# The fourth batch's side scan begun in the experts' stage, with three chunk places of layer 1's prologue left empty

## The chip, the cores and the metric

The kernel runs on one core of a Trainium2 chip (NeuronCore: TensorE or PE for matmuls, VectorE or DVE, ScalarE or ACT, GpSimd or POOL, and SyncE or SP, which here only issues DMAs). The metric is the time of one execution on the device in microseconds; less is better. Times given are medians of several executions.

## The reference

Two layers over x of shape 8 x 512 x 128 (batches, positions, features). Each layer adds to x the product of one path s and a gate g, both computed from the layer-normed x:

```
xn = layernorm(x)
s  = ssm(xn)                       # layer 0: the scan
g  = silu(experts(xn))             # layer 0: top 2 of 8 experts, gelu
x  = x + s * g
xn = layernorm(x)
s  = attention(xn)                 # layer 1: one causal head
g  = silu(mla_and_experts(xn))     # layer 1: 16 heads, then 8 small experts
x  = x + s * g
```

The scan of layer 0 is what the change moves. For each batch, with z = sigmoid(xn Wz + bz), x_ssm = xn Wx + bx, B = xn WB + bB, C = xn WC + bC, dt = softplus(xn Wdt + bdt), and A = -exp(A_log), it runs over the 512 positions with a state of 128 x 16:

```
h   = exp(dt * A) * h + x_ssm * (dt * B)
y_t = sum over the 16 states of h * C_t
out = (y * z) Wout + bout
```

## The kernel before

The program has three stages with a barrier behind each: `route` (normalization, routing, lists of tokens), `experts0` (layer 0's experts) and `layer1`. Layer 0's scan has no stage of its own: it runs beside the others, written into their loops.

**The side scan.** One batch's scan is cut into 8 chunks of two states each (`NC = 8`, `PER = 2`), and one chunk is a row of 1024 elements per partition. Class `Scan` holds the pieces. A chunk (b, k) takes, in this order: `load_rows` twice on GpSimd's DMA queue (line 212, the rows of B and of C spread over all partitions, 512 KB each), `decay` on ScalarE (line 250, two exponentials), and on VectorE `enter` (line 291, u times B), `step` (line 298, the scan instruction), `weigh` (line 308, state times C) and, from the second chunk on, `add` (line 315, into y). Ahead of a batch's first chunk stand four projections on TensorE (`project`, line 191: dt, bc, x, z), `take_dt`, `logarithm`, `take_bc` and a store of B and C to HBM (`store_bc`); behind its last chunk `gate` (lines 320 and 323), `project_out` (line 196) and `finish` (line 327), which writes the batch's finished rows.

**In the experts' stage** the work is 78 tiles m (`NT`), two for each of 39 pieces of 256 sorted rows. Tile m is `up(m)` on TensorE (line 779), `gelu(m)` on ScalarE (line 854), the product hid on VectorE (line 925, two instructions) and, two tiles later, `down` on TensorE (line 795). `turn_rows` (line 766) transposes the rows that GpSimd gathered (line 900), eight tiles ahead. Each engine has its own loop over m, and `chunk_due` and `scan_due` say which piece of the scan goes beside which tile: chunk n starts at tile 3n - 1 (`SCAN_TILE`, `TILES_A_CHUNK`), its step one tile later, its weigh two, its add three. The decays of two chunks are done together, one tile ahead of the even one. dt of batch b is projected 12 tiles before its first chunk, bc 10, x 4; the batch before it is projected out 4 tiles behind, and z 6 tiles behind. Three batches (`SCANNED = 3`) run here; the last add of batch 2 is at tile 71.

**In layer 1** the loops run over slots, 24 to a batch, from -30 (`SLOT0`) to 217. Slots below 0 are the prologue: the expert rows of batch 0 are gathered (`gather`, line 1677), combined (lines 1703 to 1713), normed, turned and projected (lines 1301, 1413, 1309, 1314), the queries get their rope (lines 1738 to 1744) and go by DMA into `q_all` (line 1091); from slot -8 on the maxima of the scores are made (line 1286 on TensorE, line 1723 on VectorE), turned (line 1297) and sent as a row (line 1133), and with slot 0 the scores begin (line 1238). The one-head attention runs beside them (`qk1` in slot -6, `scores1` in -5, `turn1` in -3, its maxima on VectorE in line 1869, its exponentials in line 1642). `keep_clock` (line 1222) issues matmuls whose result nobody reads. The scan's chunks have one place every four slots from slot -14 on (`SCAN_START`, `SCAN_STRIDE`): chunk (3, 0) at -14, (3, 1) at -10, and so on; the projections of a batch have slots of their own in `SCAN_PIECES`. Batch 3 fetches its turned rows from HBM in slot -30, projects bc in slot -28, dt in -22, x in -17 and z in -4. Batch 2's `project_out` and `finish` stand ahead of slot -30.

Of the kernel before, what the change touches and what calls it, by code (L numbers as in the profile page):

```python
# [21 lines left out]
B, L = 8, 512  # L22
# [309 lines left out]
def route(nc, sems_of_stage, bk, c, x, xs, t):  # L332
# [6 lines left out]
    with ExitStack() as own:  # L339
# [40 lines left out]
        with nc.Block() as block:  # L380
            @block.sync
            def _(sp):
# [32 lines left out]
                for b in range(SCANNED, B):  # L415
                    sp.wait_ge(s["xnt_ready"], b + 1)
                    sp.dma_start(t["xnt_d"][b], xn_t_all[:, b * L:(b + 1) * L]).then_inc(t["late_in"], 16)
                    late += 1
# [267 lines left out]
SCAN_TILE, TILES_A_CHUNK = -1, 3  # L686


def experts0(nc, sems_of_stage, bk, c, xs, ys, t):
# [4 lines left out]
    with ExitStack() as own:  # L694
# [20 lines left out]
        def chunk_due(m):  # L715

            n, rest = divmod(m - SCAN_TILE, TILES_A_CHUNK)
            return (n // NC, n % NC) if rest == 0 and 0 <= n < SCANNED * NC else None
# [10 lines left out]
        with nc.Block() as block:  # L729
# [27 lines left out]
            def _(pe):  # L757
# [42 lines left out]
                for m in range(NT + 2):  # L800
# [14 lines left out]
                    if (b := scan_due(m - 6)) is not None and b >= 1:  # L815
                        pe.wait_ge(s["xcol_ready"], turned(m))
                        scan.project("z", beside, xn_t_all[:, b * L:(b + 1) * L])
# [96 lines left out]
            def _(dve):  # L914
                v = nc.vector
                for m in range(SCAN_TILE, NT + 2):
# [89 lines left out]
def layer1(nc, sems_of_stage, bk, bank, c, x, ys, out, t):  # L1006
# [5 lines left out]
    with ExitStack() as own:  # L1012
# [84 lines left out]
        def scan_due(slot, what):  # L1097

            for b in range(SCANNED, B):
                after, bank_of = SCAN_PIECES[scan_start(b) % SLOTS][what]  # L1100
                if slot == scan_start(b) + after:
                    return b, bank_of

        def chunk_due(slot, after):

            n, rest = divmod(slot - after - SCAN_START, SCAN_STRIDE)
            return (SCANNED + n // NC, n % NC) if rest == 0 and 0 <= n < (B - SCANNED) * NC else None
# [7 lines left out]
        with nc.Block() as block:  # L1115
            @block.sync
            def _(sp):
# [5 lines left out]
                def fetch_turned(b):  # L1123
                    if b > SCANNED:
                        sp.wait_ge(scan.s["sc_zp"], b)
                    sp.dma_start(xn_ts[:, :], xnt_d[b]).then_inc(s["xts_in"], 16)
# [79 lines left out]
            def _(pe):  # L1206
# [146 lines left out]
                scan.project_out(pe, SCANNED - 1, bk(2))  # L1353
                for slot in range(SLOT0, SLOT1):
# [21 lines left out]
                    if (at := scan_due(slot, "bc")) is not None:  # L1376
                        pe.wait_ge(s["xts_in"], 16 * (at[0] - SCANNED + 1))
                        scan.project("bc", claim(at[1], scan.s["sc_bc"], at[0] + 1), xn_ts[:])
# [144 lines left out]
            def _(act):  # L1523
# [39 lines left out]
                for slot in range(SLOT0, SLOT1):  # L1563
# [14 lines left out]
                    if (at := chunk_due(slot, -1)) is not None:  # L1578
                        scan.decay(act, *at)
# [77 lines left out]
            def _(pool):  # L1657
                link = chain_of(pool, s["pool_chain"])
                g_ = nc.gpsimd
                for slot in range(SLOT0, SLOT1):  # L1660
                    if slot == SCAN_START - 7:
                        for k in range(2):
                            for what in range(2):
                                scan.load_rows(pool, SCANNED, k, what)
                    for what, ahead in ((0, 7), (1, 5)):
                        if (at := chunk_due(slot, -ahead)) is not None and at > (SCANNED, 1):
                            if at == (SCANNED, 2) and what == 0:
                                pool.wait_ge(q_in[0], 96)
                            scan.load_rows(pool, *at, what)
# [26 lines left out]
            def _(dve):  # L1696
# [54 lines left out]
                scan.finish(dve, SCANNED - 1, bk(2))  # L1751
                for slot in range(SLOT0, SLOT1):
# [3 lines left out]
                    if (at := chunk_due(slot, 0)) is not None and at != (SCANNED, 1):  # L1756
                        scan.enter(dve, *at)
                    if (at := chunk_due(slot, 1)) is not None and at != (SCANNED, 1):
                        scan.step(dve, *at)
                    if (at := chunk_due(slot, 2)) is not None:  # L1760
                        if at == (SCANNED, 1):
                            scan.step(dve, *at)
                        scan.weigh(dve, *at)
                        if at == (SCANNED, 0):
                            scan.enter(dve, SCANNED, 1)
# [245 lines left out]
```

## Time and profile before

| | |
|---|---|
| median of 3 runs | 1284.59 us (1284.12 to 1284.82) |
| profiled execution | 1283.6 us, its span 1281.8 us |
| granted TensorE clock, mean | 0.912 of full speed |
| busy share: PE, PEld, DVE, ACT, POOL | 85%, 54%, 75%, 49%, 24% |
| routing stage | to about 66 us of the span |
| experts' stage | about 67 to 329 us |
| layer 1's prologue | 329 to 404 us |

Times in rows are microseconds from the start of the span, unless marked ns. A row of the timeline has start, duration, engine, line, operation, what is written from what, how many instructions were merged, and in brackets how long the engine had been idle before and what ended that. "issue" means that the profile shows nothing that it waited for. SPq, POOLq and ACTq are the DMA issues of these engines. The chain is the work that ended last, followed back from the end.

### The profile page before, as it was taken

How to read it: one execution, taken by the hardware profiler on the slowest of the kernel's cores; microseconds unless marked ns; L12 is line 12 of the kernel's file. 1: busy time of each engine (PE TensorE's matmuls, PEld its weight loads, DVE VectorE, ACT ScalarE, POOL GpSimd, SP SyncE). 2: the span in 40 equal slices, each digit the busy share in tenths (PEclk: the TensorE clock that was granted, in tenths of full speed). 3: DMA queues.
4: the chain of work that ended last, by engine and by line, in shares of the span. 5: the costliest groups of instructions: out<-in, count | busy, mean ns of one | idle time of the engine just before them, and what ended most of it. 6: DMA issues, size and time to landing. Idle time of an engine off the chain costs nothing.

```text
span 1281.8 us, 19217 instructions
## 1 busy us (share of the span) xinstructions
PE 1094.9 (85%) x6765; PEld 691.2 (54%) x6765; DVE 960.7 (75%) x1490; ACT 623.0 (49%) x1111; POOL 305.9 (24%) x370
## 2 busy tenths in 40 slices
PE   7669999999678877889889988989997888899976
PEld 6557787788334334544544554554464455455453
DVE  6848887897367886898797898898889877655423
ACT  2647767664223534446445554654544543353521
POOL 2075554550403201310320330041032111000000
PEclk9679999999887789899988988988898988899998
DMA  7568777674344253244324425434432520320020
GB/s 194 181 216 255 229 234 224 221 232 142 109 84 112 87 115 97 91 102 114 96 77 111 115 96 114 115 98 116 104 106 87 123 58 27 59 52 19 19 50 9
DMA packets 97069, 150.24 MB, mean 117 GB/s; under 512 B 26984, under 2 KB 55984, under 8 KB 96912
## 3 DMA queue, kind: packets, MB, share of 16 engines
q1 hardware_dynamic: 73840, 72.33, 22.5%
q0 software_dynamic: 22976, 76.43, 19.3%
q8 instruction: 56, 0.92, 0.3%
q10 hardware_dynamic: 160, 0.26, 0.1%
q14 instruction: 37, 0.30, 0.1%
HBM read 124.33 MB, written 11.54 MB: 106 GB/s over the span
## 4 chain that ended last, share of the span: by engine, by line
PE 39%; DVE 18%; issue 6%; ACT 6%; DMA 4%; POOL 1%; SPq 1%; POOLq 0%; DVEq 0%; ACTq 0%
PE bank L1238 8%; PE bank L1267 3%; DVE neg_max L1723 3%; PE bank L1318 3%; PE bank L1327 3%; PE bank L1332 3%; DMA q_all<-turned_rows 2%; PE bank L1286 2%; PE bank L1244 2%; ACT probs L1533 2%; PE bank L1322 2%; DVE sc_state L298 2%; PE bank L1246 1%; PE bank L1309 1%; DVE sc_y L315 1%
## 5 line engine op out<-in xcount | busy, mean ns | idle before, releaser
L1533 ACT ACTIVATE probs<-bank 128x1024 f32<-128x1024 f32 (+1 forms) x192 | 169.3, 882 | 286.8 <-PE bank L1244 208.3
L1723 DVE TENSOR_REDUCE neg_max<-bank 128x2 f32<-128x1024 f32 (+3 forms) x256 | 203.4, 815 | 131.3 <-PE bank L1244 88.3
L1238 PE MATMUL bank<-q_all,kk 49*128 49x512 f32 (+3 forms) x1024 | 203.8, 497 | 49.0 <-ACT probs L1533 26.7
L212 POOL DMA_DIRECT2D sc_bc_wide<-scan_bc x128 | 73.1, 572 | 445.2 <-DVE sc_ub L291 241.1
L1238 PEld LDWEIGHTS bank<-q_all,kk 49*128 49x128 f32 x1024 | 86.5, 194 | 149.9 <-ACT probs L1533 54.9
L1286 PE MATMUL bank<-kr,q_all 48*128 48x512 f32 (+3 forms) x512 | 117.3, 494 | 43.9 <-DVE neg_max L1723 43.6
L779 PE MATMUL bank<-xcol,wst 128*128 128x256 f32 x624 | 149.8, 384 | 0.6 <-ACT xcol L841 0.6
L298 DVE TENSOR_TENSOR_SCAN sc_state<-sc_a,sc_ub 128x1024 f32<-128x1024 f32 x64 | 145.9, 2280 | 0.0
L900 POOL DMA_INDIRECT xrow<-sorted_in,token_of x78 | 103.9, 1332 | 117.5 <-PE bank L766 63.3
L779 PEld LDWEIGHTS bank<-xcol,wst 128*128 128x128 f32 x624 | 114.2, 193 | 13.6 <-issue 0.9
L1267 PE MATMUL bank<-probs,vaug 128*32 128x512 f32 (+3 forms) x1024 | 97.3, 477 | 0.0
L925 DVE SCALAR_TENSOR_TENSOR hid<-bank,wst,gel 128x256 f32<-128x256 f32 x156 | 67.3, 473 | 37.3 <-issue 24.0
L1286 PEld LDWEIGHTS bank<-kr,q_all 48*128 48x128 f32 x512 | 49.1, 201 | 77.0 <-DVE neg_max L1723 61.4
L291 DVE TENSOR_TENSOR sc_ub<-sc_u,sc_bc_wide 128x1024 f32<-128x1024 f32 x64 | 77.9, 1217 | 16.5 <-DMA sc_bc_wide<-scan_bc 14.7
L1677 POOL DMA_INDIRECT expert_out<-sorted_out,slot x64 | 75.9, 1187 | 55.2 <-POOLq L138 35.2
L250 ACT ACTIVATE sc_a<-sc_dt,neg_a 128x511 f32<-128x511 f32 x128 | 84.2, 711 | 5.7 <-PEq L682 4.3
L795 PE MATMUL bank<-w,hid 128*128 x624 | 84.7, 279 | 0.5 <-DVE hid L925 0.5
L795 PEld LDWEIGHTS bank<-w,hid 128*128 128x128 f32 x624 | 77.3, 191 | 11.4 <-issue 7.1
L854 ACT ACTIVATE gel<-bank,wst 128x256 f32<-128x256 f32 x156 | 64.6, 477 | 23.1 <-PE bank L779 22.0
L308 DVE TENSOR_TENSOR sc_ub<-sc_state,sc_bc_wide 128x1024 f32<-128x1024 f32 x56 | 67.9, 1213 | 0.0
L315 DVE TENSOR_TENSOR sc_y<-sc_y,sc_ub 128x1024 f32<-128x1024 f32 x56 | 67.9, 1213 | 0.0
L1692 POOL TENSOR_SCALAR mean_sq<-ssq 128x4 f32<-128x4 f32 x8 | 6.8, 853 | 184.0 <-ACT work_b L1590 184.0
(297 smaller groups left out, 1810.7 us busy)
## 6 DMA issues: line engine op xcount, KB each, us to landing
sc_bc_wide<-scan_bc POOLq DMA_DIRECT2D x128, 512.0 KB, 4.8
wst<-in_wexp SPq DMA_DIRECT2D x39, 512.0 KB, 4.7
q_all<-q_kind SPq DMA_DIRECT2D x94, 128.0 KB, 4.3
rec_wide<-head_recips SPq DMA_DIRECT2D x31, 256.0 KB
p_t<-gates_turned SPq DMA_DIRECT2D x14, 512.0 KB, 6.5
sorted_out<-xrow SPq DMA_DIRECT2D x7, 640.0 KB, 6.5
rows_all<-in_x SPq DMA_DIRECT2D x8, 256.0 KB, 4.7
sorted_in<-rows_all SPq DMA_DIRECT2D x8, 256.0 KB, 5.5
```

What stands on the lines that cost most here:

```text
L250: last = self.nc.scalar.activation(self.v["a"][:, n % 2, j, 1:L], self.v["dt"][:, 1:L], ACT.Exp, scale=self.neg_a[:, state:state + 1])
L291: self.nc.vector.tensor_tensor(v["ub"][:], v["u"][:].unsqueeze(1).to_broadcast([P, PER, L]), v["bc_wide"][:, n % 2, 0, :, :], ALU.mult).th ...
L298: self.nc.vector.tensor_tensor_scan(merged(v["state"][:]), merged(v["a"][:, n % 2, :, :]), merged(v["ub"][:]), 0.0, ALU.mult, ALU.add).the ...
L315: self.nc.vector.tensor_tensor(v["y"][:], v["y"][:], v["ub"][:], ALU.add).then_inc(s["sc_add"], 1)
L779: last = mm(bk(inner(m)[half])[:, i * ROWS:(i + 1) * ROWS], wst[:, w % WB, half * FF + f * P:half * FF + (f + 1) * P], xcol[:, w % 3, :], ...
L795: last = mm(bk(5)[:, r * P:(r + 1) * P], hid[:, m % 4, i, r * P:(r + 1) * P], w2[:, bass.ds(e * FF + f * P, P)], start=False, stop=(f == F ...
L900: nc.gpsimd.indirect_dma_start(out=xrow[:, m, :], out_offset=None, in_=xs[0:B * L], in_offset=bass.IndirectOffsetOnAxis(ap=t["token_of"][: ...
L1238: mm(bank[1][:, par, at:at + n], kk[rows, b % 2, kt * P:(kt + 1) * P], q_all[rows, quad // 2 % 3, pair, kt * P:L].bitcast(F32), start=(at ...
L1267: last = mm(bk(4)[row:row + 32, kt * P:L], vaug[:, b % 2, kt, :], probs[:, (6 * quad + 2 * kg + pr) % RING, par, at:at + L - kt * P], star ...
L1286: mm(bank[0][:, par, at:at + n], q_all[rows, quad // 2 % 3, pair, i * P:(i + 1) * P], kr[rows, b % 2, 0:n], start=(at == 0), stop=False)
L1533: af(probs[:, slot % RING, :, 0:width], bank[1][:, :, 0:width], ACT.Exp, scale=0.125).then_inc(s["p_ready"], 1)
L1723: last = v.tensor_reduce(neg_max[:, quad % 2, pr:4:2, i], bank[0][:, :, at:at + (i + 1) * P], AX, ALU.max, negate=True)
```

## The change

- `experts0` goes on with the scan: three more chunks (`EARLY = 3`), (3, 0) to (3, 2), at tiles 71, 74 and 77, with all that batch 3 needs ahead of them, and batch 2's `project_out`, `finish` and batch 3's z at tiles 75 and 77. ScalarE's decays come in pairs, so that of (3, 3) is made there too. VectorE's loop gets one more round (to m = 80), in which the last step, weigh and add stand. TensorE waits for `sc_rows` before it projects z.
- In `layer1` batch 3's fetch, projections, store, dt, logarithm, x and z are gone; only its gate and out stay. Chunk (3, 3) takes the place of (3, 0) at slot -14; the places at -10, -6 and -2 are empty; chunk (3, 4) and all behind it are where they were. GpSimd loads two rows in slot -21 instead of four. Batch 2's `project_out` and `finish` no longer stand ahead of slot -30.
- In `route` one store of turned rows less is made (four batches instead of five).

```diff
--- before.py
+++ after.py
@@ -412,7 +412,7 @@
                 sp.wait_ge(s["biases_split"], 6)
                 for part in range(3):
                     sp.dma_start(t["bias16"][part:part + 1, :], bias_part[:, part, :]).then_inc(s["rows16_in"], 16)
-                for b in range(SCANNED, B):
+                for b in range(SCANNED + 1, B):
                     sp.wait_ge(s["xnt_ready"], b + 1)
                     sp.dma_start(t["xnt_d"][b], xn_t_all[:, b * L:(b + 1) * L]).then_inc(t["late_in"], 16)
                     late += 1
@@ -683,7 +683,7 @@
 
 
 
-SCAN_TILE, TILES_A_CHUNK = -1, 3
+SCAN_TILE, TILES_A_CHUNK, EARLY = -1, 3, 3
 
 
 def experts0(nc, sems_of_stage, bk, c, xs, ys, t):
@@ -715,7 +715,7 @@
         def chunk_due(m):
 
             n, rest = divmod(m - SCAN_TILE, TILES_A_CHUNK)
-            return (n // NC, n % NC) if rest == 0 and 0 <= n < SCANNED * NC else None
+            return (n // NC, n % NC) if rest == 0 and 0 <= n < SCANNED * NC + EARLY else None
 
         def scan_due(m):
 
@@ -814,6 +814,7 @@
                         scan.project_out(pe, b - 1, beside)
                     if (b := scan_due(m - 6)) is not None and b >= 1:
                         pe.wait_ge(s["xcol_ready"], turned(m))
+                        pe.wait_ge(scan.s["sc_rows"], b)
                         scan.project("z", beside, xn_t_all[:, b * L:(b + 1) * L])
                     if m >= 2:
                         down(m - 2)
@@ -913,7 +914,7 @@
             @block.vector
             def _(dve):
                 v = nc.vector
-                for m in range(SCAN_TILE, NT + 2):
+                for m in range(SCAN_TILE, NT + EARLY):
                     if 0 <= m < NT:
                         dve.wait_ge(s["up_psum"], m + 1)
                         dve.wait_ge(s["gel_ready"], m + 1)
@@ -1097,14 +1098,18 @@
         def scan_due(slot, what):
 
             for b in range(SCANNED, B):
+                if b == SCANNED and what not in ("gate", "out"):
+                    continue
                 after, bank_of = SCAN_PIECES[scan_start(b) % SLOTS][what]
                 if slot == scan_start(b) + after:
                     return b, bank_of
 
         def chunk_due(slot, after):
 
+            if slot - after == SCAN_START:
+                return SCANNED, EARLY
             n, rest = divmod(slot - after - SCAN_START, SCAN_STRIDE)
-            return (SCANNED + n // NC, n % NC) if rest == 0 and 0 <= n < (B - SCANNED) * NC else None
+            return (SCANNED + n // NC, n % NC) if rest == 0 and EARLY < n < (B - SCANNED) * NC else None
 
         def quad_due(slot, after):
 
@@ -1121,8 +1126,7 @@
                     sp.dma_start(xt[:, b % 3, :, :], x[b].rearrange("(j p) d -> p j d", p=P)).then_inc(s["x_in"], 16)
 
                 def fetch_turned(b):
-                    if b > SCANNED:
-                        sp.wait_ge(scan.s["sc_zp"], b)
+                    sp.wait_ge(scan.s["sc_zp"], b)
                     sp.dma_start(xn_ts[:, :], xnt_d[b]).then_inc(s["xts_in"], 16)
 
                 def maximum_rows(quad):
@@ -1350,7 +1354,6 @@
                     last.then_inc(s["rec_psum"], 1)
                     down_part(B - 2, 3, bk(5)).then_inc(s["moe_psum"], 1)
 
-                scan.project_out(pe, SCANNED - 1, bk(2))
                 for slot in range(SLOT0, SLOT1):
                     quad, j = divmod(slot + LEAD, 6)
                     if 0 <= slot < SLOTS * B:
@@ -1374,7 +1377,7 @@
                     if (at := scan_due(slot, "z")) is not None:
                         scan.project("z", claim(at[1], scan.s["sc_z"], at[0] + 1), xn_ts[:])
                     if (at := scan_due(slot, "bc")) is not None:
-                        pe.wait_ge(s["xts_in"], 16 * (at[0] - SCANNED + 1))
+                        pe.wait_ge(s["xts_in"], 16 * (at[0] - SCANNED))
                         scan.project("bc", claim(at[1], scan.s["sc_bc"], at[0] + 1), xn_ts[:])
                     if (at := scan_due(slot, "dt")) is not None:
                         scan.project("dt", claim(at[1], scan.s["sc_dtr"], at[0] + 1), xn_ts[:])
@@ -1575,7 +1578,7 @@
                         scan.take_dt(act, at[0], bk(at[1]))
                     if (at := scan_due(slot, "log")) is not None:
                         scan.logarithm(act, at[0])
-                    if (at := chunk_due(slot, -1)) is not None:
+                    if (at := chunk_due(slot, -1)) is not None and at > (SCANNED, EARLY):
                         scan.decay(act, *at)
                     if due(slot, "silu0") == 0:
                         for j in range(J):
@@ -1659,13 +1662,10 @@
                 g_ = nc.gpsimd
                 for slot in range(SLOT0, SLOT1):
                     if slot == SCAN_START - 7:
-                        for k in range(2):
-                            for what in range(2):
-                                scan.load_rows(pool, SCANNED, k, what)
+                        for what in range(2):
+                            scan.load_rows(pool, SCANNED, EARLY, what)
                     for what, ahead in ((0, 7), (1, 5)):
-                        if (at := chunk_due(slot, -ahead)) is not None and at > (SCANNED, 1):
-                            if at == (SCANNED, 2) and what == 0:
-                                pool.wait_ge(q_in[0], 96)
+                        if (at := chunk_due(slot, -ahead)) is not None and at > (SCANNED, EARLY):
                             scan.load_rows(pool, *at, what)
                     if (b := due(slot, "gather")) is not None:
                         if b == 1:
@@ -1748,21 +1748,16 @@
                     dve.wait_ge(s["silu1_ready"], (MT + 1) * b + n + 1)
                     v.tensor_tensor(hm[:, n, :], bk(at), hm[:, n, :], ALU.mult).then_inc(s["hm1_ready"], 1)
 
-                scan.finish(dve, SCANNED - 1, bk(2))
                 for slot in range(SLOT0, SLOT1):
                     quad, j = divmod(slot + LEAD, 6)
                     if 0 <= quad < QUADS:
                         reduce_maxima(quad, j)
-                    if (at := chunk_due(slot, 0)) is not None and at != (SCANNED, 1):
+                    if (at := chunk_due(slot, 0)) is not None:
                         scan.enter(dve, *at)
-                    if (at := chunk_due(slot, 1)) is not None and at != (SCANNED, 1):
+                    if (at := chunk_due(slot, 1)) is not None:
                         scan.step(dve, *at)
                     if (at := chunk_due(slot, 2)) is not None:
-                        if at == (SCANNED, 1):
-                            scan.step(dve, *at)
                         scan.weigh(dve, *at)
-                        if at == (SCANNED, 0):
-                            scan.enter(dve, SCANNED, 1)
                     if (at := chunk_due(slot, 3)) is not None and at[1] >= 1:
                         scan.add(dve, *at)
                     if (at := scan_due(slot, "gate")) is not None:
```

## Rows read from the trace of the kernel before

**Rows 1.** The page, part 1: busy time, share of the span and instructions of each engine.

```profile
PE 1094.9 (85%) x6765; PEld 691.2 (54%) x6765; DVE 960.7 (75%) x1490; ACT 623.0 (49%) x1111; POOL 305.9 (24%) x370
```

**Rows 2.** VectorE's timeline: hid of tiles 29, 35, 53, 59 and 77.

```profile
176.04 0.88 DVE L925 SCALAR_TENSOR_TENSOR hid<-bank,wst,gel 128x256 f32<-128x256 f32 x2 [3.98 <-issue]
...
196.18 0.88 DVE L925 SCALAR_TENSOR_TENSOR hid<-bank,wst,gel 128x256 f32<-128x256 f32 x2 [3.80 <-PE bank L779]
...
255.02 0.88 DVE L925 SCALAR_TENSOR_TENSOR hid<-bank,wst,gel 128x256 f32<-128x256 f32 x2 [3.98 <-issue]
...
273.34 0.88 DVE L925 SCALAR_TENSOR_TENSOR hid<-bank,wst,gel 128x256 f32<-128x256 f32 x2 [1.98 <-issue]
...
321.34 0.88 DVE L925 SCALAR_TENSOR_TENSOR hid<-bank,wst,gel 128x256 f32<-128x256 f32 x2 [1.85 <-PE bank L779]
```

**Rows 3.** ScalarE's timeline between tiles 52 and 53.

```profile
249.38 2.56 ACT L250 ACTIVATE sc_a<-sc_dt,neg_a 128x511 f32<-128x511 f32 x4
...
252.80 1.28 ACT L854 ACT_TABLE_LOAD   x1
```

**Rows 4.** The chain that ended last, 329 to 353: start, duration, what.

```profile
332.88 3.81 PE bank L191 x4
...
351.08 2.07 PE bank L191 x2
```

**Rows 5.** VectorE's timeline, 343 to 392.

```profile
343.20 0.27 DVE L1703 TENSOR_SCALAR expert_out<-expert_out,gate 128x128 f32<-128x128 f32 x1
...
346.24 0.38 DVE L1786 BATCH_NORM_AGGREGATE mv<-stats 128x2 f32<-128x6 f32 x4
...
374.84 0.69 DVE L1738 TENSOR_TENSOR q_kind<-bank,cos_q 128x512 f32<-128x512 f32 x1 [3.78 <-issue]
...
379.70 2.28 DVE L298 TENSOR_TENSOR_SCAN sc_state<-sc_a,sc_ub 128x1024 f32<-128x1024 f32 x1
...
383.15 1.28 DVE L1723 TENSOR_REDUCE neg_max<-bank 128x2 f32<-128x768 f32 x2
...
389.90 1.23 DVE L1723 TENSOR_REDUCE neg_max<-bank 128x2 f32<-128x1024 f32 x1 [2.61 <-PE bank L1244]
391.05 2.28 DVE L298 TENSOR_TENSOR_SCAN sc_state<-sc_a,sc_ub 128x1024 f32<-128x1024 f32 x1
```

**Rows 6.** The timeline of ScalarE and TensorE, 394 to 405.

```profile
394.93 0.69 ACT L1642 ACTIVATE q_kind<-bank,neg_max 128x512 f32<-128x512 f32 x1 [5.08 <-DVE neg_max L1869]
...
400.99 0.41 PE L1297 MATMUL bank<-c_ident,neg_max 128*16 128x128 f32 x1
...
404.43 1.88 PE L1238 MATMUL bank<-q_all,kk 49*128 49x512 f32 x4 [1.09 <-DMA q_all<-turned_rows]
```

**Rows 7.** The timeline of SP's queue at the ends of the first two stages.

```profile
52.78 0.59 SPq L435 DMA_DIRECT2D sin_q<-in_sin  x1
67.73 0.38 SPq L736 DMA_DIRECT2D wst<-in_wexp  x1
...
325.56 0.36 SPq L742 DMA_DIRECT2D sorted_out<-xrow  x1
329.08 0.39 SPq L1121 DMA_DIRECT2D xt<-in_x  x1
```

**Rows 8.** The page, parts 5 and 6: groups with busy, mean ns; issues with landing.

```profile
L298 DVE TENSOR_TENSOR_SCAN sc_state<-sc_a,sc_ub 128x1024 f32<-128x1024 f32 x64 | 145.9, 2280 | 0.0
L291 DVE TENSOR_TENSOR sc_ub<-sc_u,sc_bc_wide 128x1024 f32<-128x1024 f32 x64 | 77.9, 1217 | 16.5 <-DMA sc_bc_wide<-scan_bc 14.7
L308 DVE TENSOR_TENSOR sc_ub<-sc_state,sc_bc_wide 128x1024 f32<-128x1024 f32 x56 | 67.9, 1213 | 0.0
...
expert_out<-sorted_out,slot POOLq DMA_INDIRECT x64, 2.6
```

**Rows 9.** GpSimd's timeline: the last of the first eight gathers.

```profile
338.50 0.95 POOL L1677 DMA_INDIRECT expert_out<-sorted_out,slot  x1 [0.30 <-issue]
```

**Rows 10.** Stretches: length, busy of PE, PEld, DVE, ACT, POOL (instructions), clock, DMA share, GB/s.

```profile
404.00:412.00 8.00, 6.67 (x26) 3.46 (x27) 5.83 (x6) 2.20 (x3) 6.48 (x6) 0.54 0.43 133
```

## The prediction

> **What bounds the kernel now.** I read the page first for the shares: TensorE 85%, VectorE 75%, ScalarE 49% busy [rows 1]. A share says nothing of one stage, so I then read the two places that the change touches: the experts' stage (about 68 to 329 us of the span) and layer 1's prologue (329 to 404 us, up to the first scores).
>
> In the **experts' stage** I followed one instruction, the VectorE product hid of each tile (line 925, two per tile), because it is what tiles are counted by. Three starts of it that lie 24 tiles apart are tile 29 at 176.04, tile 53 at 255.02 and tile 77, the last one, at 321.34 [rows 2]. The first 24 take 78.98 us, the last 24 take 66.32 us. The first stretch holds batch 1's last six chunks, batch 2's first two, and all that prepares batch 2 (dt, bc, x, z, out). The second holds batch 2's last six chunks and then nothing of a scan. The rows inside show where it costs: before a tile whose ScalarE work has a pair of decays ahead of it VectorE sits idle, 3.98 us (tile 29), 3.80 (tile 35) and 3.98 (tile 53) where a piece of the next batch is also in the way, 1.98 us where not (tile 59) [rows 2]. The rows on ScalarE say why: around tile 53 it loads a table, runs the four decays (2.56 us), takes z, loads the gelu table back (1.28 us) and only then makes gel, after which hid can start at 255.02 [rows 3]. So this stage is set in turn by VectorE, TensorE and, at each pair of chunks, ScalarE; the scan is not free in it.
>
> In the **prologue** I read the chain that ended last. It starts with the fetch of the turned rows of batch 3, two projections (3.81 us) and ScalarE's dt, behind which the first tanh of the expert outputs stands [rows 4]. Later it runs through the projection of x (2.07 us) [rows 4], the DMA of the query rows, in which VectorE sits idle 3.78 us [rows 5], and then a to and fro between TensorE's maxima and VectorE, where the scan's instructions stand in line with the maxima [rows 5].
>
> **Experts' stage, what is added.** With batch 3 begun at tile 71, tiles 53 to 77 do what tiles 29 to 53 do today, instruction for instruction: dt at 59, bc at 61, x at 67, decays at 70, gate at 71, out at 75, decays and z at 76 and 77. So I take 78.98 for 66.32: **+12.66 us** [rows 2]. This includes the projections, ScalarE's work with its table loads (ten in the first stretch, four in the second), the store of bc on SP's queue and the row loads on GpSimd's, since today's stretch has all of them too. The new wait of z for the finished rows of batch 2 stands on TensorE at tile 77; down 75, 76 and 77 are queued behind it. The rows are finished at tile 75 on VectorE, two tiles earlier, so it costs nothing; were they late, VectorE's own queue would be, which the 12.66 counts. Two corrections. At tile 76 no rows are left to turn, so the chain to the last gel is shorter by the turning and its copy; about 0.9 us less is my estimate, from ScalarE's small gaps there. The other is the tail. Today hid 77 starts at 321.34, the last store is issued at 325.56 and layer 1 starts at 329.08 [rows 7], 7.74 us after hid. After the change VectorE still has, behind hid (0.88) [rows 2], an add, an enter, a scan step, a weigh and an add: 1.21 + 1.22 + 2.28 + 1.21 + 1.21 = 7.1 us by the means (an add is as long as a weigh) [rows 8], 8.0 us in all. Then come the barriers; I put 1.1 of the 3.5 us between the last store's issue and layer 1 down to them and the rest to the store, an estimate. That is 9.1 instead of 7.74, **+1.4**. Sum: 12.66 - 0.9 + 1.4 = **+13.2 us** until layer 1 starts. Bounds: if the two ends of the tail hide each other wholly, and tile 76 saves 1.5, 11; if nothing is saved, 14.
>
> The Trainium skill ("ScalarE: Activation LUTs", Table sets: the hidden batching unit) says to batch activations by table set, since a change of set costs a load each time. The trace agrees: 1.28 us per load [rows 3]. By that page's 1283 ns the six loads more between gelus would cost 7.7 us, if all lay on the path, and with them alone in place of the 12.66 the time would be 1285.5; the 12.66 of the rows has them in it already.
>
> **Routing stage.** One of five stores of turned rows is gone from SP's queue. SP's last issue there is at 52.78 and its first of the next stage at 67.73 [rows 7], so nothing is won: 0.
>
> **Prologue, what is removed.** (a) Fetch, bc, store, dt and logarithm are gone. The first tanh no longer waits. What is late next is the gather of expert rows: eight of them on GpSimd's queue, the last at 338.50 [rows 9], landing 2.6 us later by the median [rows 8], 341.1. From the last combine (343.20) to the aggregate (346.24) VectorE needs 3.04 us today [rows 5], so the aggregate starts at about 344.2: **-2.0**. (b) The x projection stands between the two turnings on TensorE: 2.07 us [rows 4], at 1.2 GHz. The clock came up only later, behind this work, so with less of it ahead more of the keys' product may run at the lower level; I take **-1.6**, bounds 1.0 (all of the half clock handed on) and 2.1. (c) Chunk 3's enter, step and weigh fall into VectorE's idle time before 374.84 [rows 5], at no cost; without that cover they would be 4.7 us. Its load of rows goes out right behind the gathers on GpSimd's queue and waits for nothing. But its add now stands between the second rope and the first maximum, +1.2. (d) Behind it, today's line is reduce, step, weigh, reduce: the step starts at 379.70 and the second reduce at 383.15 [rows 5]. Without them the second reduce starts when TensorE's matmuls are done, 381.8 with the 1.2 of the add in it: -1.35. The step at 391.05 [rows 5] holds back the four maxima of the other attention; ScalarE's exponentials behind them start at 394.93 [rows 6]. Without it they end with their matmuls, at about 391.5: -3.4 in all. TensorE's turning waits for those exponentials, and behind it the maxima are turned at 400.99; then DMA, and the scores at 404.43 [rows 6]. With z's projection gone too, TensorE is late next, and I get -3.7 at the turned maxima, and so at the first scores. (e) Chunk 3's place at slots -2 to 1 is empty, but TensorE and ScalarE are the chain there: nothing. The sum of (a), (b) and (d) is 2.0 + 1.6 + 3.7 = **7.3 us** won; bounds 3.5 (if (b) and half of (d) go to other waits) and 9. From slot 2 on the program is the same.
>
> **Sum.** +13.2 - 7.3 = **+5.9 us**. Against the profiled execution's own 1283.6 (span 1281.8 and 1.8 around it) this is 1289.5; the median of the runs shown is 1.0 above that execution, so 1290.5.
>
> **Rivals.**
> *VectorE is the bound of the prologue* (ends faster). Of the 17.7 us of three chunks, 5.9 each by the means, all but one enter (that one runs in idle time today) lie behind 378; less the added add that is 15.3. If each microsecond were on the path, the gain would be 2.0 + 1.6 + 15.3 = 18.9, and the time 1284.6 + 13.2 - 18.9 = 1278.9. It decides from a prologue gain above 13.2. For it: step and reduce stand back to back at 379.70 to 383.15. Against: VectorE waits for TensorE before 389.90, 2.61 us [rows 5], so part of what goes turns into such waits. Chance 0.05.
> *TensorE's clock stays up in the prologue.* At 404 to 412 it was granted 0.54 of full speed [rows 10], and the scores' first four matmuls took 1.88 us [rows 6]. If fewer waits kept it at 2.4 GHz, each such piece on the path would be shorter by 1 us; I count up to six (x's place, keys, latents, the other attention's projections, two scores), an estimate. Net 0: 1284.5. Against: the wait for the DMA before the scores stays, and so do the gaps in which the clock falls. Chance 0.10.
> *The last tiles hide the scan.* With no rows left to turn and no gather, tiles 71 to 77 might wait for nothing but VectorE; the added stage then costs 3.7 less (one stall like the 3.98 of tile 53): 1286.8. Chance 0.11.
> *The prologue gives back little.* If the query rows' DMA or TensorE at half clock takes the place of the scan, only 3.5 of 7.3 comes: 1294.3. Chance 0.14.
> *The forecast*: chance 0.60, own range 1288 to 1293.
>
> **How the numbers follow.** The likeliest is 1290.5. The range goes from 1285.5 to 1294.5: it leaves out the first rival and the second where it is whole. About 0.2% (2.6 us) is what a measurement of this kernel can tell from no change. Faster: 0.05 of the first rival and 0.02 of the second, 0.07. Within: 0.07 of the second and 0.07 of the third, 0.14. Slower: 0.79.
>
> **What would show it.** In the changed profile hid 77 should start at about 333 to 334, with stalls of 3.8 us before tile 59 and 3 to 4 before tile 77; VectorE should end the stage with sc_y, and layer 1's fetch start at 342.3. The first aggregate should lie 15.1 us behind the start of layer 1 (17.2 today), and the first scores 68 (75.35 today). I am wrong if hid 77 starts before 330, or if the first scores come more than 13 us earlier against layer 1's start than today.

## The result, and the profile after

The changed kernel takes 1296.1 us (median of 20 runs, 1282.5 to 1300.7) where the kernel before takes 1284.7 in the same series: a ratio of 1.0080, 95% interval 1.0061 to 1.0099, so about 10.3 us slower (7.8 to 12.7); the two medians lie 11.4 apart. Forecast was 5.9 slower, with a range of 1285.5 to 1294.5: the sign is right, the size forecast is a little over half of the measured one, and the time lies outside the range. All times and ratios are of fast executions; the one slow execution, of early2 below, took 1423.3 us at a granted clock of 0.72.

The page of the changed kernel, part 1, answers to [rows 1]. The instructions of TensorE and VectorE are as many as before, and all shares stay within a point:

```profile
PE 1107.1 (85%) x6765; PEld 698.9 (54%) x6765; DVE 962.5 (74%) x1490; ACT 628.0 (48%) x1116; POOL 304.4 (23%) x370
```

VectorE's timeline gives the same tiles as [rows 2]; here are tile 29, tile 53 and tile 77, and behind tile 77 the tail of the stage, which is new:

```profile
179.01 0.88 DVE L926 SCALAR_TENSOR_TENSOR hid<-bank,wst,gel 128x256 f32<-128x256 f32 x2 [3.98 <-issue]
...
257.96 0.88 DVE L926 SCALAR_TENSOR_TENSOR hid<-bank,wst,gel 128x256 f32<-128x256 f32 x2 [3.98 <-issue]
...
336.05 0.87 DVE L926 SCALAR_TENSOR_TENSOR hid<-bank,wst,gel 128x256 f32<-128x256 f32 x2 [3.10 <-issue]
336.84 1.21 DVE L315 TENSOR_TENSOR sc_y<-sc_y,sc_ub 128x1024 f32<-128x1024 f32 x1
338.15 1.22 DVE L291 TENSOR_TENSOR sc_ub<-sc_u,sc_bc_wide 128x1024 f32<-128x1024 f32 x1
339.41 2.29 DVE L298 TENSOR_TENSOR_SCAN sc_state<-sc_a,sc_ub 128x1024 f32<-128x1024 f32 x1
341.74 1.23 DVE L308 TENSOR_TENSOR sc_ub<-sc_state,sc_bc_wide 128x1024 f32<-128x1024 f32 x1
343.00 1.23 DVE L315 TENSOR_TENSOR sc_y<-sc_y,sc_ub 128x1024 f32<-128x1024 f32 x1
```

Tiles 29 to 53 take 78.95 us, for 78.98 before. Tiles 53 to 77 take 78.09 instead of 66.32. The last store and layer 1's first fetch, on SP's queue and in the whole timeline, answer to [rows 7]:

```profile
339.59 0.36 SPq L742 DMA_DIRECT2D sorted_out<-xrow  x1
...
345.68 0.39 SPq L1126 DMA_DIRECT2D xt<-in_x  x1
```

The store is issued 3.54 us behind hid 77 (4.22 before), but VectorE works until 344.23, and layer 1 starts 1.45 us behind that.

In the prologue, VectorE's timeline around the second rope answers to the fourth to sixth of [rows 5]:

```profile
389.48 0.69 DVE L1738 TENSOR_TENSOR q_kind<-bank,cos_q 128x512 f32<-128x512 f32 x1 [6.37 <-DMA q_all<-q_kind]
...
393.21 1.22 DVE L315 TENSOR_TENSOR sc_y<-sc_y,sc_ub 128x1024 f32<-128x1024 f32 x1
394.34 1.22 DVE L1723 TENSOR_REDUCE neg_max<-bank 128x2 f32<-128x1024 f32 x1
396.99 1.29 DVE L1723 TENSOR_REDUCE neg_max<-bank 128x2 f32<-128x768 f32 x2 [1.43 <-PE bank L1250]
```

The place of the scan step between two reduces is now a wait for TensorE of 1.43 us, and the add stands ahead of the first, as the prediction had it. But VectorE waits 6.37 us for the query rows.

This profiled execution took 1300.65 us, 4.5 above the median of its kernel, so its differences are not all the change's. The traces of the other runs, below, tell them apart. Here is each trace in pieces, worked out from starts in the timelines: tile 0, tiles 53 to 77, from hid 77 to the start of layer 1 (the fetch of x on SP's queue), and, counted from that start, the first aggregate (mv), the first product with cos_k (kk), the first and second rope, the first maximum, the first scores; last what remains of the span behind the first scores.

| trace | hid 0 | 53 to 77 | tail | mv | kk | rope 1 | rope 2 | maximum | scores | rest |
|---|---|---|---|---|---|---|---|---|---|---|
| before | 81.4 | 66.32 | 7.74 | 17.2 | 28.8 | 32.3 | 45.8 | 49.5 | 75.4 | 877.4 |
| again_before | 81.5 | 66.34 | 7.61 | 17.2 | 29.0 | 32.5 | 45.9 | 49.6 | 75.5 | 877.2 |
| after | 83.5 | 78.09 | 9.63 | 15.1 | 25.4 | 28.9 | 43.8 | 48.7 | 70.9 | 882.0 |
| again_after | 81.0 | 78.13 | 9.63 | 15.1 | 25.1 | 28.6 | 45.6 | 50.5 | 72.1 | 877.0 |
| guarded | 81.0 | 78.10 | 9.62 | 15.2 | 25.5 | 29.0 | 42.1 | 47.0 | 68.9 | 873.3 |
| early2 | 83.5 | 74.90 | 7.07 | 15.2 | 24.5 | 28.0 | 40.8 | 45.7 | 69.4 | 874.8 |
| early1 | 83.8 | 73.20 | 8.47 | 15.1 | 24.8 | 28.3 | 41.5 | 46.4 | 70.2 | 871.4 |
| early0 | 83.7 | 70.91 | 8.46 | 15.1 | 24.3 | 27.8 | 40.2 | 43.9 | 68.7 | 869.0 |
| short_vector | 81.4 | 77.04 | 7.43 | 15.1 | 24.7 | 28.1 | 45.0 | 49.9 | 70.4 | 874.2 |
| short_decay | 81.6 | 75.23 | 9.62 | 15.2 | 25.0 | 28.5 | 44.7 | 49.5 | 71.5 | 870.8 |
| prefetch | 84.3 | 66.32 | 7.73 | 15.0 | 25.9 | 29.4 | 42.4 | 46.1 | 73.4 | 875.6 |
| prefetch_x | 84.7 | 66.34 | 7.59 | 15.0 | 25.3 | 28.8 | 42.3 | 46.0 | 71.9 | 873.7 |

### The profile page after: what moved, and what is told of

Same layout as the page of the kernel before. It is cut to its first block, busy times and chain, and to the rows that moved or that the text cites. A ratio compares the mean times of both kernels' runs of the same rounds, so it can differ in the third digit from the quotient of the medians.

```text
span 1298.6 us, 19225 instructions
## 1 busy us (share of the span) xinstructions
PE 1107.1 (85%) x6765; PEld 698.9 (54%) x6765; DVE 962.5 (74%) x1490; ACT 628.0 (48%) x1116; POOL 304.4 (23%) x370
## 4 chain that ended last, share of the span: by engine, by line
PE 38%; DVE 19%; issue 6%; ACT 4%; DMA 4%; POOL 1%; SPq 1%; another core or an unknown queue 0%; DVEq 0%; POOLq 0%; ACTq 0%
PE bank L1242 8%; DVE neg_max L1723 4%; PE bank L1271 3%; PE bank L1322 3%; PE bank L1331 3%; PE bank L1336 2%; PE bank L1290 2%; PE bank L1326 2%; PE bank L1248 2%; DVE sc_state L298 2%; ACT probs L1536 2%; PE bank L1250 2%; DVE sc_y L315 2%; DMA q_all<-turned_rows 1%; PE bank L1313 1%
## 5 line engine op out<-in xcount | busy, mean ns | idle before, releaser
L779 PEld LDWEIGHTS bank<-xcol,wst 128*128 128x128 f32 x624 | 114.5, 194 | 13.7 <-issue 0.9
L926 DVE SCALAR_TENSOR_TENSOR hid<-bank,wst,gel 128x256 f32<-128x256 f32 x156 | 67.3, 472 | 39.5 <-issue 28.1
L795 PEld LDWEIGHTS bank<-w,hid 128*128 128x128 f32 x624 | 78.0, 193 | 15.7 <-issue 11.8
L1677 POOL DMA_INDIRECT expert_out<-sorted_out,slot x64 | 75.4, 1178 | 39.1 <-POOLq L138 20.0
```

The lines of the kernel that those rows point to most:

```text
L779: last = mm(bk(inner(m)[half])[:, i * ROWS:(i + 1) * ROWS], wst[:, w % WB, half * FF + f * P:half * FF + (f + 1) * P], xcol[:, w % 3, :], ...
L795: last = mm(bk(5)[:, r * P:(r + 1) * P], hid[:, m % 4, i, r * P:(r + 1) * P], w2[:, bass.ds(e * FF + f * P, P)], start=False, stop=(f == F ...
```

## The experiments

Each ran in five rounds beside the kernel before on the same chip; ratios are to it.

**The change and the kernel before once more** (no edit).

> The changed kernel once more, for a second trace. The account so far: tiles 53 to 77 cost 11.8 us more than before, the tail of the experts' stage 1.9, the prologue gives back 4.5, and the 3.0 us in the routing stage and the 4.7 us behind the first scores that the first trace also shows are chance (TensorE's granted clock). It expects hid 53 to hid 77 at 78.1 us, layer 1's start to the first scores at 70.9, and 877 to 880 us behind the first scores. The rival, that the change also slows the steady part of layer 1, expects 881 to 883 there again.

> The kernel before once more, for a second trace and to see what two timings of one kernel differ by. Expected: a ratio of 1.000 with an interval of some 0.003, hid 53 to hid 77 at 66.3 us, layer 1's start to the first scores at 75.4. If the part behind the first scores (877.4 us in the first trace) comes out 3 us or more otherwise here, such differences are chance; if it is 877 again, the rival of a slower steady part gains.

The change: 1.0101 (1.0052 to 1.0151). The kernel before against itself: 0.9989 (0.9953 to 1.0024), so two such series differ by 0.1% with nothing changed, and the interval is 0.35% to either side. Tiles 53 to 77, the tail and the parts up to the first rope repeat to 0.5 us. The rest behind the first scores is 877.0 in the change's second trace and 877.2 in the second of before: the 4.7 us more in the change's first trace were chance, and so were the 2.1 us by which its tile 0 started later. The rival of a slower steady part falls. The first scores were expected at 70.9 in the change's second trace and came at 72.1. Between the ropes the two traces of the change differ, 14.9 and 17.0 us, where the two of before agree on 13.45: something there is unsteady in the change.

**Both without layer 1.** Of each kernel all of layer 1 is left out, and a copy of x stands in its place. The edit, shortened:

```diff
-        layer1(nc, sems_of_stage, bk, bank, c, x, ys, out, locals())
+        sp.dma_start(out, x[0:B]).then_inc(copied, 16)      # in a block of its own
```

> The kernel before with layer 1 left out: a copy of x to the output stands in its place, so the scan's later chunks and all of layer 1 are not computed. Expected: layer 1's place starts at 329 us of the span, so some 335 us in all. It is the base of cut_after.

> The changed kernel with layer 1 left out in the same way. If the added stage time is the tiles' 11.8 and the tail's 1.9, it is 13.7 us above cut_before. My forecast had 13.2. If a part of the 16.6 us by which layer 1 starts later in the first trace were due to the routing stage's one store less, the difference would be nearer 16.6.

340.21 us (339.3 to 341.0; about 335 was expected) and 353.85 (352.8 to 356.6): **13.64 us** more. The stage's price is thus measured by itself, in time and not only in a trace, and it is the 11.8 of the tiles and the 1.9 of the tail. The routing stage has no part in it: in the traces of these two kernels tile 53 starts at 253.92 and 253.95 us, and what stands in layer 1's place 13.72 us later in the second.

**How the price is made up: fewer early chunks.** A new table gives the places; batch 3's projections and the rest are as in the change. The edit, shortened (EARLY is 0, 1 or 2; the table's row for 1 and for 2 stands behind the mark #):

```diff
-SCAN_TILE, TILES_A_CHUNK, EARLY = -1, 3, 3
+SCAN_TILE, TILES_A_CHUNK, EARLY = -1, 3, 0              # 1, 2
+PLACES = {-14: 0, -10: 1, -6: 2, -2: 3}                 # {-14: 1, -6: 2, -2: 3}, {-14: 2, -6: 3}
+                            if at == (SCANNED, max(EARLY, 1) + 1) and what == 0:
+                                pool.wait_ge(q_in[0], 96)
```

> One part of the change alone: batch 3's projections, bc store, dt, logarithm, x, u, z and batch 2's out go to the experts' stage, and all four first chunks stay in the prologue in their old places. By the rows of before (tiles 53 to 59 cost 1.8 more with dt ahead, 59 to 65 cost 0.7 more, then x, dt, gate and out some 1.5) the stage gets 3 to 5 us longer, with no tail, since hid is VectorE's last long work; the prologue gives back the 3.5 us of the tanh and of x. Expected: 0 to 1.5 us above before. If the preparation were the costly part, it would be 8 or more above.

> The change with one early chunk instead of three (the decays of two are made early): chunk 1 in the first place of the prologue, the second place empty, chunks 2 and 3 in the last two. Against early0 the stage gets one stall behind a pair of decays (2 us) and 1 to 2 us on VectorE, the prologue gives back the first scan step behind the rope, 1.4 us. Expected: 2 to 4 us above before. If each early chunk costs a third of the whole, it is about 3.8 of 11.4.

> Two early chunks, the third in the prologue's first place, the fourth in its third place. No second pair of decays is made early, so the stall of 3.1 us before tile 77 and the tail of 1.9 us aren't there. Expected: 3 to 6 us above before. The theory that the cost sits in the second pair of decays and in the tail wants a step of 5 us or more between this and the change; if cost goes evenly with chunks, it is some 7.6 above before and the step is 3.8.

Ratios 1.0019 (0.9989 to 1.0049), 1.0019 (0.9984 to 1.0053) and 1.0035 (1.0001 to 1.0069). The times alone can't tell the first two from no change. The traces can say where layer 1 starts: tiles 53 to 77 and the tail together are 74.0 us before, 79.4 with no early chunk, 81.7 with one, 82.0 with two and 87.7 with three. So the preparation costs 5.4, the first early chunk 2.3, the second 0.3 (1.7 more in the tiles, 1.4 less in the tail), and **the third 5.7** (3.2 in the tiles, 2.6 in the tail). That is the step of 5 us or more which the theory of the second pair of decays and the tail had asked for; an even price per chunk would have given 3.8. early2 was forecast at 3 to 6 above and lies at 4.5, early1 at 2 to 4 and lies at 2.4, early0 at 0 to 1.5, measured 2.4, with an interval that holds both.

Two forecasts about early0 missed. Its stage gets 5.4 us longer, not 3 to 5, of which 0.7 is in the tail, where nothing was expected. And its prologue gives back 6.7 us (75.4 to 68.7), not 3.5, although all four chunks still stand there; guarded, below, with three of them gone, gets to 68.9. 1.2 us of that lie ahead of kk (24.3 for 25.5), where the granted clock differs too: in the ten us from 15 us behind layer 1's start it is 0.62 in early0 and 0.51 in guarded. One trace of each can't say how much the empty places are worth, but these two show no gain from them at the first scores beyond what the moved preparation gives.

**Which engine holds the tiles.** First VectorE's part of the three early chunks is left out but for 8 columns, then ScalarE's decays of the four chunks (the fourth's come with the third's) but for 7 columns. The edits, shortened:

```diff
+        w = 8 if b == SCANNED and k < EARLY else L          # in enter, step, weigh and add
```

```diff
+            early = b == SCANNED and k <= EARLY             # in decay
+            w = 8 if early else L
+            ... ACT.Gelu if early else ACT.Exp ...
```

> The change, with the VectorE instructions of the three early chunks cut to 8 columns (that part of the scan is not computed); ScalarE's and TensorE's work for them, the table loads and the DMAs stay. If VectorE's 17 us for the chunks set the stage, most of the added time goes: hid 53 to hid 77 falls from 78.1 to about 70 and the tail from 9.6 to 7.8, 8 to 10 us below the change. If the stalls behind the decays set it, it falls by 3 to 5 us only, of which 1.9 is the tail.

> The change, with the early decays (chunks 0 to 3 of batch 3) as gelus of 7 columns, so that their exponentials and the table loads around them fall away; VectorE's work stays whole (the scan's decay factors are wrong for these chunks). Cutting VectorE's early chunks gave back only 1.1 us of tiles 53 to 77 and 2.2 of the tail. If ScalarE's pairs of decays with their table loads set the added time, hid 53 to hid 77 falls from 78.1 to 72 to 74 here. If the two engines cover for each other (whichever is cut, the other sets it), it stays at 76 to 77.

With VectorE's part gone the tiles take 77.04 instead of 78.1 and the tail 7.43 instead of 9.63, 3.3 us in all. That is the 3 to 5 expected if the stalls behind the decays set the stage; the 8 to 10 that VectorE's bound had wanted don't come. ScalarE's timeline of this kernel shows what holds tile 77 then:

```profile
323.77 1.28 ACT L250 ACT_TABLE_LOAD   x1
325.07 2.56 ACT L250 ACTIVATE sc_a<-sc_dt,neg_a 128x511 f32<-128x511 f32 x4
328.26 0.38 ACT L851 ACTIVATE xrow<-bank 128x256 f32<-128x256 f32 x1 [0.64 <-PE bank L800]
328.54 0.68 ACT L240 ACTIVATE sc_z<-bank,half_bz 128x512 f32<-128x512 f32 x1
329.24 1.28 ACT L860 ACT_TABLE_LOAD   x1
330.53 0.84 ACT L860 ACTIVATE gel<-bank,wst 128x256 f32<-128x256 f32 x2
```

It is the line of [rows 3] again, load, four decays, copy, z, load, gel: 7.6 us for one tile, with VectorE's scan out of the way. With the decays cut short instead, and six table loads between tiles 53 and 77 where the change has ten, these tiles take 75.23, 2.9 less, between the two forecasts (72 to 74, or 76 to 77). There the second pair waits for VectorE:

```profile
324.62 0.48 ACT L252 ACTIVATE sc_a<-sc_dt,neg_a 128x7 f32<-128x7 f32 x2
327.47 0.49 ACT L252 ACTIVATE sc_a<-sc_dt,neg_a 128x7 f32<-128x7 f32 x2 [2.37 <-DVE sc_state L300]
```

So of the 11.8 us in the tiles 1.1 go when VectorE's part is cut, 2.9 when ScalarE's is, and the other 7.8 with neither cut; 4.6 of them are there with no early chunk at all (early0: 70.91 against 66.32). That the remaining 3.2 stay because each engine covers for the other fits the wait of 2.37 us, but a kernel with both cut, which would show it, was not run. The ratios, 1.0058 (1.0024 to 1.0092) and 1.0082 (1.0051 to 1.0113), can't be told from each other or from the change's.

**Why the prologue gave back so little.** In the kernel before, the third chunk's load waits until the first query rows have landed. The change took that line out with the place of the chunk. Guarded puts a wait back in front of chunk 4's loads:

```diff
                         if (at := chunk_due(slot, -ahead)) is not None and at > (SCANNED, EARLY):
+                            if at == (SCANNED, EARLY + 1) and what == 0:
+                                pool.wait_ge(q_in[0], 96)
                             scan.load_rows(pool, *at, what)
```

> The changed kernel with one wait put back on GpSimd's queue: the loads of chunk 4's rows, and so chunk 5's rows and the eight gathers of batch 1 queued behind them, go out only when the first query rows have landed, as in the kernel before. Theory: with three places empty that queue ran ahead, and its transfers now share the DMA engines with the query rows, so that from the first rope to the second it takes 14.9 and 17.0 us in the two traces of the change (13.5 before, 12.4 to 13.2 with fewer early chunks). Expected with the wait: 12.4 to 13.5, first scores 67 to 69.5 us behind layer 1's start (70.9 and 72.1), 2 to 4 us below the change. Rival: the query rows' landing varies by itself or by the clock; then the first rope to the second stays at 15 to 17.

The ratio is 1.0061 (1.0030 to 1.0093), between the change's and no change; the time is some 2 us better than the change's 1.0080, which these intervals alone would not carry. The trace does: from rope to rope it takes 13.1 us (12.4 to 13.5 was expected, 15 to 17 by the rival that the landing varies by itself), and the first scores come at 68.9 (67 to 69.5 expected). GpSimd's timeline shows the cause. First again_after, then guarded:

```profile
362.40 1.20 POOL L212 DMA_DIRECT2D sc_bc_wide<-scan_bc  x2
377.23 0.54 POOL L212 DMA_DIRECT2D sc_bc_wide<-scan_bc  x1 [13.63 <-DVE sc_ub L291]
378.08 2.06 POOL L1677 DMA_INDIRECT expert_out<-sorted_out,slot  x1 [0.31 <-issue]
...
387.97 0.95 POOL L1677 DMA_INDIRECT expert_out<-sorted_out,slot  x1 [0.30 <-issue]
```

```profile
384.96 1.73 POOL L212 DMA_DIRECT2D sc_bc_wide<-scan_bc  x3 [23.14 <-DMA q_all<-q_kind]
387.00 1.06 POOL L1679 DMA_INDIRECT expert_out<-sorted_out,slot  x1 [0.30 <-issue]
```

In the change the queue has little to wait for: chunk 4's rows go out at 362.40, the first of chunk 5's two loads as soon as chunk 3's enter is done (377.23), and the eight gathers of batch 1 right behind, from 378.08 to 388.9. The query rows are in flight just then, from 377 to 389, and the second rope stands behind them. guarded holds back the loads of both chunks and the gathers together, so it doesn't show which of the two the query rows meet. ScalarE and VectorE of again_after and VectorE of guarded, in this order:

```profile
389.00 0.60 ACT L1557 ACTIVATE q_kind<-bank 128x512 f32<-128x512 f32 x1 [9.02 <-DMA q_all<-q_kind]
389.00 0.69 DVE L1738 TENSOR_TENSOR q_kind<-bank,cos_q 128x512 f32<-128x512 f32 x1 [8.47 <-DMA q_all<-q_kind]
```

```profile
384.76 0.69 DVE L1740 TENSOR_TENSOR q_kind<-bank,cos_q 128x512 f32<-128x512 f32 x1 [4.60 <-DMA q_all<-q_kind]
```

All traces agree: in the four without the wait (after, again_after, short_vector, short_decay) it is 14.9, 17.0, 16.9 and 16.2 us from rope to rope, in the eight that have it 12.4 to 13.5.

**The part that was worth moving.** The first thing that the change removed from the prologue was a fetch. Moved alone, it adds only a DMA to the experts' stage. The edits, shortened (TensorE's first projection of batch 3 then waits for `turned_in`):

```diff
+                    if m == 60:                              # experts' stage, SP
+                        sp.wait_ge(scan.s["sc_u"], SCANNED)
+                        sp.dma_start(t["scan"]["xn_t"][:, :], t["xnt_d"][SCANNED]).then_inc(t["turned_in"], 16)
...
-                    if (at := scan_due(slot, "fetch")) is not None:
+                    if (at := scan_due(slot, "fetch")) is not None and at[0] > SCANNED:
```

and for prefetch_x also

```diff
                         rows_to_t(claim(6, s["xrt_ready"], b + 1), xr, "xrt_psum")
+                    if (at := scan_due(slot, "x")) is not None and at[0] == SCANNED:
+                        scan.project("x", claim(at[1], scan.s["sc_u"], at[0] + 1), xn_ts[:])
...
-                        if b == 0:
-                            keep_clock(bk(3), 3)
                         pe.wait_ge(s["xrt_ready"], b + 1)
```

> The kernel before with one thing moved: batch 3's turned rows are fetched during the experts' stage, at tile 60, into the tile that batch 2's x has left. No work is added to that stage. The first tanh should come 3.7 us earlier, and the gathers be late next, so the first aggregate lies 15.1 us behind layer 1's start instead of 17.2, as in the changed kernel, and 2 us are won, without the 13.6 that the change pays. Tiles 53 to 77 should stay at 66.3.

> As prefetch, and x's projection of batch 3 stands behind the second turning instead of before it, in place of three matmuls that only keep the clock. Expected: keys' product 1 to 1.5 us earlier than in prefetch (25.5 us behind layer 1's start, 28.8 before), 3 to 3.5 us below before in all.

Ratios 0.9952 (0.9925 to 0.9980) and 0.9953 (0.9926 to 0.9979): 1276.78 and 1275.69 us where before has 1279.91 in the same series. Both are faster than the kernel before, if by less than 1%; the second edit adds nothing that shows in the time. By the ratios that is 6.1 us (2.6 to 9.6) and 6.0 (2.7 to 9.5), by the medians 3.1 and 4.2, where 2 and 3 to 3.5 were expected; the first scores come 2.0 and 3.5 us earlier than before, and what the ratios have beyond that the traces don't account for. Tiles 53 to 77 stay at 66.3 us, and ScalarE's first tanh comes at 340.66, 7.95 us behind layer 1's start (10.7 before):

```profile
340.13 0.63 ACT L230 ACTIVATE sc_log_dt<-sc_log_dt 128x512 f32<-128x512 f32 x1
340.66 0.49 ACT L1588 ACTIVATE grow<-expert_out 128x128 f32<-128x128 f32 x2
```

That is 2.8 us earlier, where 3.7 was expected. The first aggregate is at 15.0, behind the gathers, and the change with all its work moved came no further at this spot: 15.1. kk in prefetch_x comes 0.6 us earlier than in prefetch, at 25.3 (25.5 expected).

## Why the prediction was half right

**The stage: right.** 12.66 - 0.9 + 1.4 = 13.2 was forecast, 13.64 is measured. Reading the 24 tiles of the next batch off the 24 of the last one gave 11.76 with the small correction, and the traces have 11.77 to 11.79. The tail was a little short: 9.63 us for 9.1, because VectorE needs 8.18 us from hid 77 on, not 8.0, and layer 1 starts 1.45 us behind its end, not 1.1. The rival "the last tiles hide the scan" fell with hid 77's stall of 3.10 us.

**(a) and (b): right.** The first aggregate was forecast at 15.1 us behind layer 1's start and is at 15.1. kk comes 3.4 us earlier in the first trace (28.8 to 25.4) and 3.9 in the second (29.0 to 25.1), for 2.0 + 1.6.

**(c): the step that failed.** It says that chunk 3's load "goes out right behind the gathers on GpSimd's queue and waits for nothing", and stops there. That is true of chunk 3's load, but the same question had to be put to everything behind it on that queue, and the working has no term for it. The queue was held by two things before: by the enters of the chunks in the places now empty, and by the wait for the query rows, a line that the diff removes and that the working never priced. Without them chunk 5's load and eight gathers meet the query rows: 14.9 and 17.0 us between the ropes in the two traces, +1.5 and +3.6 where the forecast has nothing. guarded shows it: with the wait back, 13.1. I had even named "the query rows' DMA" as a wait that might take the scan's place, with a chance of 0.14, but as something that lies there anyway, not as something that the change makes longer.

**(d): right in sign, somewhat too large.** From the first maximum to the first scores 4.9 us were to go (3.7 net, with the add's 1.2 ahead of it), and 3.7, 4.2 and, in guarded, 4.0 went. The three projections of the other attention take longer now: 4.0 us from the first start to the last end before, 5.4 in the change's first trace, 4.5 in its second and 5.0 in guarded, which is about what is missing in each. The second and third of them in TensorE's timeline of before, then of the change:

```profile
387.01 1.33 PE L1473 MATMUL bank<-xn_t,c_wk 128*128 128x512 f32 x2
388.17 1.05 PE L1476 MATMUL bank<-c_wv,xn_t 128*128 128x128 f32 x8
```

```profile
400.85 1.92 PE L1476 MATMUL bank<-xn_t,c_wk 128*128 128x512 f32 x2
402.56 1.92 PE L1479 MATMUL bank<-c_wv,xn_t 128*128 128x128 f32 x8
```

The granted clock is 0.52 from 399 to 405 us, for 0.74 from 385 to 390 in before. guarded, without the late query rows, still needs 21.9 us from the first maximum to the first scores, so this is not their doing. That the lost waits would raise the clock, the second rival, did not happen: over the prologue it is 0.80 in both traces of before, 0.77 and 0.76 in the change's and 0.79 in guarded. Why it is lower was not tested. And early0 leaves open how much of (d) is the scan's doing: from the first rope to the first scores it is 43.1 us before, 40.9 in early0, which has every scan step in its old place but not z's projection, and 39.9 in guarded, which has the steps away too.

**The sum.** 13.64 less the 4.5 and 3.4 us of the two traces is 9.1 and 10.2, where 13.2 - 7.3 = 5.9 was forecast; the time shows 10.3 (7.8 to 12.7). The fourth rival, that the prologue gives back only 3.5 of the 7.3, came nearest in its number, 1294.3. With the wait of (c) left in it would be 13.7 - 6.6 = 7.1, which is guarded (7.8 by its ratio, 3.8 to 11.9).

**The range.** It was built from the trace's price of each step, and reached to 1294.5 by taking half of the gain away. Its own bounds, 14 for the stage and 3.5 for the prologue, add up to more, 1284.6 + 10.5 = 1295.1, and the measurement's own scatter was left out: the runs of the kernel before spread over 12 us (1278.0 to 1290.1), and the difference of two series of twenty carries an interval of 2.5 us to either side.

## What to carry to other kernels

When a step is taken out of a loop, read its queue downwards: what else did its waits hold back, and which transfer is in flight when that goes out, with an engine waiting for it? The period of a regular stage that has the same work in it, read off the trace, priced the added work in the tiles to 0.9 us here, and to 0.1 with the estimate for the turning that is missing at the end. The price of a chunk is not even: the one that brings the next pair of table loads and ends behind the stage's last store cost 5.7 us where the one before it cost 0.3. And before work is moved to win a wait, look whether moving the fetch alone wins it: here that made 0.48% faster what the whole move made 0.8% slower.

## What the runs showed of the hardware that I had not expected

Tiles 29 to 53 take 78.95 to 78.99 us in all twelve traces of whole kernels, while the part of layer 1 behind the first scores took 869 to 882 us. Tile 0 starts at 81 or at 84 us, in traces with the change and without it. The routing stage shows one source of that: the 32 small matmuls of line 470 take 4.89 us in the trace of before and 7.01 in the change's first, but 4.79 in the change's second, so it goes with the execution and not with the kernel. The granted clock of the stretch does not explain it, since it is 0.65 in the faster one:

```profile
34.00:41.00 7.00, 7.00 (x36) 6.32 (x36) 4.04 (x10) 4.48 (x12) 0.00 (x0) 0.65 1.03 323
```

```profile
34.00:42.00 8.00, 8.00 (x38) 7.83 (x38) 3.99 (x10) 4.60 (x10) 0.00 (x0) 1.00 1.02 323
```

The first is of before, the second of the change's first trace; the columns are those of [rows 10]. What makes the difference stays open.
